# Routed rows summed by accumulating gathers in SBUF, their shares carried with the sorted rows

## The reference

```python
xn = layernorm(x)
out = x + attention(xn) + moe(xn)

# attention: 16 heads, latent queries (128) and keys/values (64), rotary part 64, causal softmax
attn = softmax(causal(query @ key.T * scale)); y = (attn @ value) @ W_o
# moe
scores = sigmoid(xn @ gate_w)
topk_w, topk_i = top_k(scores, 6)              # 6 of 32 experts per token
topk_w = topk_w / sum(topk_w)                  # the shares
combine = one_hot(topk_i) * topk_w             # (token, expert)
routed = einsum('tef,efd,te->td', silu(xn @ wg) * (xn @ wu), wd, combine)
shared = silu(xn @ sg) * (xn @ su) @ sd
```

## Time and profile before

| what | us |
|---|---|
| three runs | 1430.83, 1434.82 (median), 1435.81 |
| profiled execution, its time | 1436.87 |
| its span, first to last instruction | 1434.7 |
| first heads | 192.59 to 610.73 |
| experts | 610.73 to 960.09 |
| last heads | 960.09 to 1431.5 |
| PE, DVE, ACT, POOL busy in the span | 1302.8, 938.8, 851.0, 588.7 |
| mean granted TensorE clock (1 is 2.4 GHz) | 0.977 |

### The profile page before, as it was taken

How to read it: one execution, slowest core, us unless ns; L and a number is a source line. 1 busy time by engine, 2 the same in 40 slices (tenths; PEclk the granted TensorE clock), 3 DMA queues, 4 the chain that set the end, 5 groups by cost and what they waited for, 6 DMA issues and landing times. The chain is left out here.

```text
span 1434.7 us, 24478 instructions
## 1 busy us (share of the span) xinstructions
PE 1302.8 (91%) x7385; PEld 963.7 (67%) x7385; DVE 938.8 (65%) x3727; ACT 851.0 (59%) x2294; POOL 588.7 (41%) x607
## 2 busy tenths in 40 slices
PE   4899769999999999889999999988899898998996
PEld 3566446777776777677888888865566666666664
DVE  3578678777777777423664333327888888888784
ACT  1455437677666667445566666646666666666663
POOL 1111127776676777400000000014666666566663
PEclk8899979999999999999999999989999999999998
DMA  9776652323228222298855555532233332332321
GB/s 345 309 266 249 247 201 96 111 82 107 100 82 301 103 96 78 70 286 310 268 179 177 177 176 179 177 121 70 85 101 85 103 107 78 107 107 78 107 74 56
DMA packets 133844, 216.98 MB, mean 151 GB/s; under 512 B 14743, under 2 KB 108631, under 8 KB 128855
## 3 DMA queue, kind: packets, MB, share of 16 engines
q1 hardware_dynamic: 101462, 152.48, 31.2%
q0 software_dynamic: 18432, 50.36, 10.8%
q10 hardware_dynamic: 13824, 12.59, 2.8%
HBM read 103.70 MB, written 111.67 MB: 150 GB/s over the span
## 5 line engine op out<-in xcount | busy, mean ns | idle before, releaser
L1708 ACT ACTIVATE l_prob<-l_prob,l_negmax 128x512 f32<-128x512 f32 (+3 forms) x256 | 142.1, 556 | 154.3 <-DVE l_negmax L1794 154.2
L1063 POOL DMA_INDIRECT sorted_x<-f_xn_row,slot_no x192 | 204.5, 1065 | 49.9 <-issue 49.3
L1219 ACT ACTIVATE f_prob<-f_prob,f_negmax 128x512 f32<-128x512 f32 (+3 forms) x256 | 142.6, 558 | 122.0 <-DVE f_negmax L1292 120.0
L1601 PE MATMUL ps<-l_kt,l_qt 128*128 128x512 f32 (+3 forms) x512 | 176.9, 452 | 39.1 <-DVE l_qt L1772 22.4
L1539 POOL DMA_INDIRECT l_rows<-sorted_y,slot_no x192 | 185.6, 967 | 49.1 <-issue 41.6
L2126 DVE TENSOR_TENSOR act_f<-hidden,ps 128x96 f32<-128x96 f32 x224 | 56.9, 254 | 211.1 <-ACT hidden L2101 210.3
L2063 PE MATMUL ps<-wgu_sb,xt_e 128*128 x896 | 185.0, 329 | 7.5 <-ACT xt_e L2096 7.5
L1122 PE MATMUL ps<-kt_s,f_qt 128*128 128x512 f32 (+3 forms) x512 | 170.4, 447 | 5.7 <-DVE f_qt L1283 4.4
L1292 DVE CUSTOM_DVE_ANT_0 f_prob<-ps,mask_add 128x512 f32<-128x512 f32 (+3 forms) x256 | 121.0, 486 | 81.0 <-issue 80.1
L1794 DVE CUSTOM_DVE_ANT_0 l_prob<-ps,mask_add 128x512 f32<-128x512 f32 (+3 forms) x256 | 122.0, 485 | 71.8 <-issue 70.6
L2063 PEld LDWEIGHTS ps<-wgu_sb,xt_e 128*128 128x128 f32 x896 | 141.0, 191 | 10.1 <-issue 9.9
(11 more groups left out here) (202 smaller groups left out, 2940.1 us busy)
## 6 DMA issues: line engine op xcount, KB each, us to landing
sorted_x<-zeros SPq DMA_DIRECT2D x14, 2048.0 KB, 8.9
rows_in<-sorted_x SPq DMA_DIRECT2D x112, 256.0 KB, 3.0
sorted_y<-rows_out SPq DMA_DIRECT2D x112, 256.0 KB, 2.1
wgu_sb<-in_wgu SPq DMA_DIRECT2D x16, 384.0 KB, 5.3
x_in<-in_x SPq DMA_DIRECT2D x8, 512.0 KB, 9.7
xn_dram<-xn SPq DMA_DIRECT2D x8, 512.0 KB, 3.7
base_dram<-x_in SPq DMA_DIRECT2D x8, 512.0 KB, 2.9
nqt_dram<-nqt_out SPq DMA_DIRECT2D x8, 512.0 KB, 3.9
```

Of the source, the lines that this page charges most:

```text
L1063: pool.indirect_dma_start(sorted_x, bass.IndirectOffsetOnAxis(ap=slot_no[:, t, k:k + 1], axis=0), xn_row[buf][:], None).then_inc(scattered ...
L1219: act.activation(prob[:, i, qt, 0:w], prob[:, i, qt, 0:w], ACT.Exp, bias=negmax[:, i, qt:qt + 1], scale=-1.0, accum_out=rowsum[:, g // 2 % ...
L1601: mm = pe.matmul(s_ps[k % 2][:, 0:w], qt[g // 2 % 2][g % 2][:, n * P:w], kt[b - HB][:, 0:w], start=True, stop=True)
L1708: act.activation(prob[:, i, qt, 0:w], prob[:, i, qt, 0:w], ACT.Exp, bias=negmax[:, i, qt:qt + 1], scale=-1.0, accum_out=rowsum[:, g // 2 % ...
```

## The change

The sorted rows become 288 wide: 256 values and the token's 32 shares. POOL writes the shares behind the loaded rows before it scatters them (one product with ones per tile). The zero fills grow with the rows (2304 columns each for 2048). In the experts DVE multiplies `hidden * share * up` in one instruction; the share is the column of the tile's expert, so DVE reads the expert into a register as PE does. `find_shares` is gone. A load of rows now waits for `act_done` of pair r-1, since the share is read until then.

In the last heads the gathers write with `compute_op=add` on top of the base in SBUF. A group is a batch (eight groups, 4, 0, 5, 1, ...), loaded as one 512 KB tile `sums` in eight steps; four buffers. Gather m of 24 adds choice k = m // 4 of token tile t = m % 4, and waits until the one before on the same token tile has landed. DVE has no sums, no merge and no copy of the first half: it adds `sums` where it copied. ACT stores whole groups for batches 0 to 3. DVE now copies 512 of the 1280 columns of the transposed probabilities, as in the first heads.

```diff
@@ head @@
-GATHERED = [*range(GT, NT), *range(GT)]
-PACE = 2
-ZCOLS = 2048
+GROUPS = [b for j in range(HB) for b in (HB + j, j)]
+HW = H + NE
+ZCOLS = 2304
...
-        sorted_x = dram("sorted_x", (NTILE * P, H))
+        sorted_x = dram("sorted_x", (NTILE * P, HW))
...
-        self.rows_in = [ctx.enter_context(nc.sbuf_tensor(f"rows_in{i}", [P, 2, H], F32)) for i in range(self.AHEAD)]
+        self.rows_in = [ctx.enter_context(nc.sbuf_tensor(f"rows_in{i}", [P, 2, HW], F32)) for i in range(self.AHEAD)]
...
@@ heads_first, POOL @@
                     pool.wait_ge(row_loaded[buf], 16 * (t // ROWS) + 16)
+                    pool.tensor_tensor(xn_row[buf][:, H:HW], comb[:, t, :], one[:].to_broadcast([P, NE]), ALU.mult)\
+                        .then_inc(shares_put, 1)
+                    pool.wait_ge(shares_put, t + 1)
                     pool.tensor_tensor(carrier[:, buf:buf + 1], one[:], one[:], ALU.mult)
...
@@ heads_last @@
-        def gathered_tile(self, g, lag):
...
+        def group(self, g):
+
+            n, step = divmod(NH * (self.now - HB) + g, GROUP)
+            return (n, step) if 0 <= n < len(GROUPS) else (None, step)
...
-                for k in range(HALFK * half, HALFK * (half + 1)):
-                    pool.indirect_dma_start(rows[par][:, k, :], None, sorted_y,
-                                            bass.IndirectOffsetOnAxis(ap=slot_no[:, GATHERED[c], k:k + 1], axis=0))\
-                        .then_inc(gathered[par], 16)
+            def gather(n, m):
+
+                k, t = divmod(m, TT)
+                chain = gathered[n % 2][t]
+                if k == 0 and t == 0:
+                    pool.wait_ge(base_loaded[n % NSUM], 16 * (n // NSUM) + 16)
+                if n >= 2 or k > 0:
+                    pool.wait_ge(chain, 16 * (TOPK * (n // 2) + k))
+                pool.indirect_dma_start(sums[n % NSUM][:, t, :], None, sorted_y,
+                                        bass.IndirectOffsetOnAxis(ap=slot_no[:, TT * GROUPS[n] + t, k:k + 1], axis=0),
+                                        compute_op=ALU.add).then_inc(chain, 16)
...
-                act.activation(pt[:, g % 2, 0:PT_W], pt_ps[:, 0:PT_W], ACT.Copy).then_inc(pt_act, 1)
+                act.activation(pt[:, g % 2, 512:PT_W], pt_ps[:, 512:PT_W], ACT.Copy).then_inc(pt_act, 1)
...
-                dve.scalar_tensor_tensor(total[par][:], rows[par][:, k, :], share[:, c, k:k + 1],
-                                         (base if k == 0 else total)[par][:], ALU.mult, ALU.add).then_inc(totalled, 1)
...
+            def turned(b, g):
+                dve.wait_ge(pt_ready, turns(b) + g + 1)
+                dve.tensor_copy(pt[:, g % 2, 0:512], pt_ps[:, 0:512]).then_inc(pt_dve, 1)
...
+                if rnd == 0:
+                    for t in range(2 * tp, 2 * tp + 2):
+                        dve.wait_ge(gathered[0][t], 16 * TOPK * (b - HB + 1))
...
-                if rnd == 0:
-                    dve.tensor_copy(tiles, acc_ps).then_inc(res_added, 1)
-                else:
-                    dve.tensor_tensor(tiles, acc_ps, x_res[:, 2 * tp:2 * tp + 2, :], ALU.add).then_inc(res_added, 1)
...
+                base = sums[2 * (b - HB) % NSUM][:, 2 * tp:2 * tp + 2, :] if rnd == 0 else tiles
+                dve.tensor_tensor(tiles, acc_ps, base, ALU.add).then_inc(res_added, 1)
...
@@ sorted_tiles @@
-                    sp.wait_ge(xt_ready, 2 * r + (2 - 2 * AHEAD))
+                    sp.wait_ge(act_done, 2 * r + (2 - 2 * AHEAD))
...
+                def read_experts(j):
+                    first = ITER // 4 * i + j // 4
+                    read[j // 4] = dve.value_load(words[0:1, bass.ds(first, 1)], min_val=0, max_val=ALL_LAST)
...
+                        share = rows_in[(j - 1) // 2 % AHEAD][:, 1 - par, bass.ds(H + expert_of(j - 1), 1)]
                         dve.wait_ge(silu_done, c + 1)
-                        dve.tensor_tensor(act_f[1 - par][:], hidden[1 - par][:], gu_ps[1 - par][:, FE:2 * FE],
-                                          ALU.mult).then_inc(act_done, 1)
+                        dve.scalar_tensor_tensor(act_f[1 - par][:], hidden[1 - par][:], share,
+                                                 gu_ps[1 - par][:, FE:2 * FE], ALU.mult, ALU.mult).then_inc(act_done, 1)
...
-                    if i in (1, 2) and par == 0:
-                        last.find_shares(dve, PAIRS * (i - 1) + j // 2, comb, slot_of, slot_top)
```

169 lines of the change are left out of this document (62 added, 107 removed).

## The result

The change made the kernel slower. Six runs of each on one chip: 1445.93 us median (1440.66 to 1448.81) for 1435.32 (1430.18 to 1438.04), a ratio of 1.0075 with a 95% interval of 1.0046 to 1.0104. The forecast was 1386 us. The profiled execution took 1447.72 us with a span of 1446.0.

The account below looks back on a forecast made before the run. PE bounds the experts; DVE's and ACT's extra work lengthens the last heads. -56.3 + 3.0 + 4 = -49.3 us gives a profiled time of 1387.6, about 1386 us as median; 8 in 10: 1376 to 1412.

Parts of the forecast that it names:

- Gathers, 0 us: Last heads: at the plain gather's price, each gather's wait for the fourth before it is over before POOL comes: 0 us.
- Its own sign of being wrong: Last heads: PE waiting for the spread or the low latents would show the forecast wrong.
- The same comes if its issue on POOL costs 1.9 us for 1.25: Last heads rival: POOL's gathers set the step; chance 0.05 beyond the tie, 0.06 for part of it, 1395 to 1427.
- Last heads as the first, -56.3: Last heads take the first heads' length, -53.3 us, and lose 3.0 us more for a disturbance only the first have.
- Cover on POOL: In all 64 steps POOL has over a quarter of its time free, which hides the 32 share products.
- Experts, loads, +4, bounds 0 to +9: Experts' crowded start: wider row loads cost 3.6 us and go out about 1.4 us later; +4 us taken.
- Experts, DVE, 0: Experts: the product's third operand and register steps use 0.2 to 0.3 us of cover, so 0 on the path.
- the cover of 0.5 us: Experts: time between the end of DVE's product and PE's load of its result; without it each 0.1 us costs 22.
- Zero fills, +3.0: Before the first heads: 12.5% more bytes in the early fills delay a store DVE waits for; +3.0 us, bounds 0 and 5.
- Share products, 0: POOL's added products of a few tenths each: 2.3 us of cover against about 2, so 0, at most +1 us.

Follow-up runs that it names:

- narrow_early: Changed kernel with 256-wide rows, no shares carried, row loads waiting for PE's transposes as before, and DVE's product reading ones (weighting left out): 1428.12 us, ratio 0.9931.
- load_early_wide: Changed kernel, rows still 288 wide, row loads waiting for PE's transposes as before, and DVE's product reading ones (weighting left out): 1432.74 us, ratio 0.9969.
- spread_on_act: Changed kernel with the last heads' spreads on ACT, low latents still on POOL, and store before load in the experts: 1413.0 us, ratio 0.9844.
- spread_on_pool: Changed kernel with the last heads' low latents on DVE behind its sum, spreads still on POOL, and store before load in the experts: 1401.83 us, ratio 0.9752.
- low_on_vector: Changed kernel with the 32 low latents of the last heads worked out by DVE and not by POOL: 1414.07 us, ratio 0.9851.

## Why the prediction was wrong

- **Gathers, 0 us: the step that failed.** I took the plain gather's 947 ns on POOL for the accumulating one, and looked for its cost in the landing, against a chain with over 7 us to spare. The landing is 3.9 us (2.8 before), and no chain waits: that part held. But POOL's part is 1.55 to 1.6 us, and the term measured +44.2 us (458.9 - 414.7). Its own sign of being wrong did show: PE waited 8.1 us for the low latents and 4.0 us for a spread (3.7 and 1.5 in the kernel before). The prediction even had the sum: "The same comes if its issue on POOL costs 1.9 us for 1.25". It is 1.85 from start to start. By that arithmetic, 192 x 1.85 + 32 x (1.27 + 1.04) = 429 us of POOL and, with the 25 us outside the steps, a stage of 454; it was 458.9. What failed was the weight: the clause got a share of 0.11 together with the landings, though no row showed such a gather, and the bound from above was never put into the range.
- **Last heads as the first, -56.3: right.** With plain gathers the stage is 414.7 us for a forecast of 415.1, a batch 98.9 us for 98.8, and PE busy 402.3 us for "near 404". One thing the prediction didn't see stood in its own: the sums on DVE took 719 ns on average where the first of each tile took 481. The difference is DVE standing still beside POOL, some 40 us (31 x 1.02 + 16 x 0.52), and it can come back wherever DVE and POOL both have such instructions.
- **Cover on POOL.** I wrote that over a quarter of POOL's time was free. That counts busy time only. Busy it was for 280 us, but 192 gaps of 0.30 us between gathers, 58 us, are POOL's time as well. 280 + 58 + 192 x 0.6 = 453 us don't fit into a stage of 415. The chance for POOL as the bound hung on that one sum.
- **Experts, loads, +4, bounds 0 to +9: measured +12 to +13.** It is 365.2 - 352.0, late and wide for early and narrow, or 363.9 - 352.0 with the mean of the three late, wide ones. "SP's next store is queued behind that wait, but it becomes due at the same time" is where it went wrong. Due at the same time is the harm: the store's data then stand behind 288 KB of load. I priced the load's bytes (3.6 us; measured about 1 in the stages, up to 6 by the medians) and took its shorter lead as nearly covered (at most 3 us, 356.0 - 352.9), but I left out the store's place in the queue (8 us).
- **Experts, DVE, 0: measured +2.6.** The product took 0.31 us as forecast, but the register steps take 0.25 us between the Silu's end and it, where I put 0.1. PE waited for `act_f` only 0.4 us in the changed kernel, its weight loads 1.7, so it wasn't the cover of 0.5 us that ran out. Through which instruction the 0.7% come I can't say.
- **Zero fills, +3.0: right.** Nine kernels with wide fills start the first heads at 194.6 to 197.2 us (mean 196.0), four with narrow ones at 191.9 to 192.7 (192.4): +3.6. The way there is less sure. DVE's wait, from which the term was worked out, is 13.12 us where I had said 14.4, so it grew by 1.7; where the rest arises wasn't traced.
- **Share products, 0: right.** The first heads take 420.1 us on average with them and 419.9 without; the 3.7 us between the two profiled executions lie within what one varies by.
- From 740 to 940 us the DMA share is 0.56 in narrow_early and 0.62 in load_early_wide. If half of the 0.56 is loads, that is 0.06 / 0.28 = 21% more for the loads, where they carry 12.5% more bytes. By the Trainium skill, DMA: Bandwidth & Descriptors, "How a descriptor splits into AXI transactions", rows of 1152 bytes take an estimated 19% more beats than rows of 1024, which would make the prediction's term of 3.6 us 5.4 (not 5.3). The trace agrees in direction and, for this pair, in size. The pair with the late load gives 0.58 and 0.67, 31% by the same sum, so the share holds something else as well and doesn't settle the figure.

The sign came from the two misses together: -56.3 + 44 of the last heads left -12.5 (the long sums included), and the experts took 15.8.

## What to carry to other kernels

An operation that moves to another engine has to be priced in that engine's issue time as well as in its landing; where no row shows it, multiply its count by twice the nearest row as a trial and see whether the engine still has a gap. When a load is made to wait for a later step, look at what else is due in its queue at that moment, and put the transfer whose buffers are the fewer in front. Where one engine is full, moving a step of some 1 us off it can gain several times its length, and which step it is matters more than a plain sum of times says: here 2 us remained with one left in place and 15 with the other. Look at what the step does to its neighbours, on its own engine and on the one beside it.

## What the runs showed of the hardware

- An indirect gather that adds to its rows in SBUF takes POOL 1531 to 2011 ns (median 1547) and lands in 3.9 us; the same gather without adding, in the same place, took 1057 ns on average and landed in 2.9 us. With 128 rows of 1 KB each, POOL's queue made twice the packets for the same bytes. Plain, then adding:

```profile
q0 software_dynamic: 18432, 53.50, 11.9%
```

```profile
q0 software_dynamic: 36864, 53.50, 18.1%
```

- DVE's sum of two SBUF tiles, 64 x 512, takes 0.69 us. Where it meets a low latent on POOL, which also reads two SBUF tiles, it takes 1.95 to 3.09 us in the changed kernel (16 sums) and 2.16 to 2.18 in spread_on_act (15), and ends about 0.57 us behind POOL's instruction. Where less than 0.1 us of the low latent was left at the sum's start, it kept its 0.69 us. No accumulating gather is needed for it. In the kernel before, a sum of 128 x 256 that takes 0.48 us took 1.50 beside a low latent (31 times), also where POOL had been idle ahead of it, and ended 0.28 us behind it. Beside a spread, which reads `rinv` and a constant, both broadcast, it took 1.00 us (16 times). In spread_on_pool and low_on_vector no sum came out long, but there no sum of the queries ran at the same time as a spread, so these two runs don't speak for the spread. How it comes about that the sums of 3.06 us started 0.65 us ahead of POOL's instruction isn't known.
- In the changed kernel the first gather behind a low latent took 1.81 us and more (1.55 after other gathers), and the next gather started 2.11 to 2.24 us after it rather than 1.85. Why wasn't traced.
- The profile's own share of the chain that ended last tells such a change at once. The line is the changed kernel's; in the kernel before DVE had the 18% and POOL 0%.

```profile
POOL 18%; PE 7%; issue 4%; DVE 1%; ACT 1%; POOLq 0%; ACTq 0%; DVEq 0%
```
